# Token numbers and router bias added on TensorE, ranks moved between z's halves, b2 added in one operation

## The reference

```python
h = layernorm(x) * (1 + ca) + sa
xi = silu(h @ Win + bin)                  # 256 channels; then a scan with decay 0.9
x = x + ga * (scan(xi) @ Wout + bout)
h = layernorm(x) * (1 + cb) + sb
logits = h @ Wr + br                      # 8 experts
probs, idx = top_k(softmax(logits), 2); probs /= probs.sum()
for each row and each of its two experts e:
    t = layernorm(relu(h @ W1[e] + b1[e])) * g1[e] + be1[e]
    y = layernorm(relu(t @ W2[e] + b2[e])) * g2[e] + be2[e]
x = x + gb * (sum of probs * y)
```

## Time and profile before

| | us |
|---|---|
| three runs | 504.31, 505.99, 506.33 (median 505.99) |
| profiled execution | 503.4 |
| span of its instructions | 501.6 |
| busy in it: PE, DVE, ACT, POOL | 475.5, 452.2, 406.3, 348.3 |

### The profile page before, as it was taken

One profiled execution on the slowest core, in us unless ns is written; L12 is line 12 of the kernel. 1 busy time (PEld: TensorE's weight loads), 2 busy tenths in 40 slices (PEclk: granted clock), 3 DMA queues, 4 the chain that ended last, 5 costly groups with the idle time before them and its releaser, 6 DMA issues. The chain is left out here.

```text
span 501.6 us, 15039 instructions
## 1 busy us (share of the span) xinstructions
PE 475.5 (95%) x3083; PEld 366.6 (73%) x3083; DVE 452.2 (90%) x2245; ACT 406.3 (81%) x1118; POOL 348.3 (69%) x461
## 2 busy tenths in 40 slices
PE   7998999999999899999999999999999999999994
PEld 6454555555567688888888888888888888888851
DVE  6879999998888899899998899999999999999994
ACT  3678898988865777777887888989998889989883
POOL 1003666666767777788888878888887888888871
PEclk9999999999999999999999999999999999999998
DMA  5990511114211578988726986766667667667555
GB/s 165 313 256 18 132 50 48 43 56 106 64 43 56 136 172 163 166 246 205 192 82 160 200 221 137 204 192 185 202 183 178 186 191 207 166 181 212 189 177 167
DMA packets 80364, 78.36 MB, mean 156 GB/s; under 512 B 11433, under 2 KB 73052, under 8 KB 80276
## 3 DMA queue, kind: packets, MB, share of 16 engines
q1 hardware_dynamic: 71860, 60.48, 48.9%
q0 software_dynamic: 8416, 16.93, 9.5%
HBM read 55.20 MB, written 22.62 MB: 155 GB/s over the span
## 5 line engine op out<-in xcount | busy, mean ns | idle before, releaser
L704 POOL DMA_INDIRECT expert_rows<-rows_ring,slot x128 | 123.4, 964 | 93.2 <-issue 74.7
L732 POOL DMA_INDIRECT expert_results<-y,target x119 | 120.4, 1012 | 32.7 <-issue 28.1
L1686 PE MATMUL bank<-W,h2T 128*128 x720 | 96.4, 277 | 1.8 <-DVE wmod L1455 0.9
L1686 PEld LDWEIGHTS bank<-W,h2T 128*128 128x128 f32 x720 | 87.5, 191 | 12.5 <-issue 5.6
L1668 PE MATMUL bank<-W1hi,h3hi 128*128 x135 | 65.5, 485 | 1.3 <-DVE h3lo L1221 1.3
L949 ACT ACTIVATE v<-wmod 128x128 f32<-128x128 f32 x135 | 41.8, 310 | 29.3 <-DVE vg L1466 25.5
L1226 DVE BATCH_NORM_STATS2 stf<-h1T 128x6 f32<-128x512 f32 x90 | 59.2, 658 | 0.0
L814 ACT ACTIVATE n<-X,nm,rs 128x128 f32<-128x128 f32 x128 | 52.7, 488 | 7.1 <-DVE nm L1395 7.1
L961 ACT ACTIVATE sde<-mve,eps 128x2 f32<-128x2 f32 (+1 forms) x138 | 40.6, 295 | 17.9 <-DVE mve L1479 15.6
L1676 PE MATMUL bank<-ident_wr,h1T 128*128 128x128 f32 x360 | 54.4, 274 | 0.2 <-ACT third_rT L829 0.2
L829 ACT ACTIVATE h2T<-bank 128x512 f32<-128x512 f32 x90 | 52.7, 586 | 1.0 <-PE bank L1676 0.9
(11 more groups left out here) (253 smaller groups left out, 1172.0 us busy)
## 6 DMA issues: line engine op xcount, KB each, us to landing
shifts<-expert_shifts SPq DMA_DIRECT2D x119, 192.0 KB
hrow<-expert_rows SPq DMA_DIRECT2D x135, 65.0 KB
xi<-expert_results SPq DMA_DIRECT2D x12, 512.0 KB, 6.0
out_x<-X SPq DMA_DIRECT2D x15, 256.0 KB, 3.9
X<-in_L_attn_x SPq DMA_DIRECT2D x7, 512.0 KB, 7.4
b_ring<-b_two_parts SPq DMA_DIRECT2D x135, 4.0 KB
W1lo<-in_L_ffn_W SPq DMA_DIRECT2D x4, 512.0 KB, 5.9
expert_rows<-rows_ring,slot POOLq DMA_INDIRECT x128
```

Of the source, the lines that this page charges most:

```text
L704: nc.gpsimd.indirect_dma_start(out=rows_d, out_offset=bass.IndirectOffsetOnAxis(ap=slot[q][:, n // TOPK, n % TOPK:n % TOPK + 1], axis=0), ...
L732: nc.gpsimd.indirect_dma_start(out=results_d, out_offset=bass.IndirectOffsetOnAxis(ap=target[i % TARGETS][:], axis=0), in_=y[k], in_offset ...
L1686: ins = mm(acc, rT[i % DEPTH][:, ch * P:(ch + 1) * P], W2[:, bass.ds(e * CF + ch, 1), :], start=(ch == 0), stop=(ch == CF - 1))
```

## The change

The row in `rows` now has h first, then token number and expert, then the logits. `ident_wr` gets two zero columns between identity and `wr` (138 columns). A new table `tags` holds per row the token number, a zero and br. Two matmuls with the identity as weights add it to the product of L1768 in the banks, so that ScalarE's two copies bring token numbers and finished logits; VectorE's addition of br and its copy of the token numbers go. `max` and `max_index` read `rows` and wait for `rows_ready`; the pieces of `scale_w2` and the table that stood between logits and `max` now stand ahead of that wait. GpSimd's wait for `logit_ready` becomes one for `best_ready`. The ranks become a function; in steps 3 to 15 it is called between the halves of z, from step 16 on where they stood. `copy_sums` is one addition over 98 partitions and stands after the experts' numbers are written; two matmuls with `padding` in step 0 fill bank 4 for it. VectorE makes `tags` with a copy and two memsets in the setup and a copy of br in step 1.

```diff
+        tags = sb("tags", [P, NT, TAGS + E])
@@ ScalarE
-                    nc.scalar.activation(rows[k2][:, 0:J - 1, TAGS:], back, ACT.Copy)
-                    nc.scalar.activation(rows[k2][:, J - 1:J, TAGS:], back_last, ACT.Copy).then_inc(rows_ready, 1)
+                    nc.scalar.activation(rows[k2][:, 0:J - 1, :], back, ACT.Copy)
+                    nc.scalar.activation(rows[k2][:, J - 1:J, :], back_last, ACT.Copy).then_inc(rows_ready, 1)
@@ GpSimd
-                pool.wait_ge(logit_ready, b + 2)
+                pool.wait_ge(best_ready, b + 2)
@@ VectorE, setup
-            vec.tensor_copy(token[:], token_i[:])
+            vec.tensor_copy(tags[:, :, 0], token_i[:])
+            vec.memset(tags[:, :, 1], 0.0)
+            vec.memset(ident_wr[:, P:P + TAGS], 0.0)
@@ gains_setup
+                dve.wait_ge(gains_loaded, 80)
+                vec.tensor_copy(tags[:, :, TAGS:], br[:].rearrange("p (o e) -> p o e", o=1).broadcast_to([P, NT, E]))
@@ copy_sums
-                for rows_k in side_rows:
-                    ins = vec.tensor_tensor(w2_sums[rows_k, n, :], bank[4][rows_k, n * D:(n + 1) * D], b2_rows[rows_k, n, :], ALU.add)
+                ins = vec.tensor_tensor(w2_sums[0:side_rows[-1].stop, n, :], bank[4][0:side_rows[-1].stop, n * D:(n + 1) * D],
+                                        b2_rows[0:side_rows[-1].stop, n, :], ALU.add)
@@ VectorE, mixer_step
-                if on(s - SUMS_FROM - 1, ROUNDS):
-                    copy_sums(s - SUMS_FROM - 1)
-                if on(c, B):
-                    dve.wait_ge(rows_ready, c + 1)
-                    vec.tensor_tensor(logit[p][:], rows[k3][:, :, LOGITS],
-                                      br[:].rearrange("p (o e) -> p o e", o=1).broadcast_to([P, J, E]),
-                                      ALU.add).then_inc(logit_ready, 1)
...
-                    dve.wait_ge(logit_ready, c + 1)
+                    dve.wait_ge(rows_ready, c + 1)
...
-                    vec.tensor_copy(rows[k3][:, :, 0], token[:, tiles(c)])
...
-                    vec.tensor_copy(rows[k3][:, :, 1], besti[p][:, :, 0]).then_inc(ids_ready, 1)
+                    vec.tensor_copy(rows[k3][:, :, D + 1], besti[p][:, :, 0]).then_inc(ids_ready, 1)
+                if on(s - SUMS_FROM - 1, ROUNDS):
+                    copy_sums(s - SUMS_FROM - 1)
@@ TensorE, gains (step 0)
+                for n in range(ROUNDS):
+                    mm(bank[4][:, n * D:(n + 1) * D], ident[:], padding[:, H], start=True, stop=True)
@@ TensorE, mixer_step
-                if on(s - 3, B):
-                    acc = ...          # the ranks, here in every step
+                if on(s - 3, B) and s >= B:
+                    ranks(s, p)
...
                     mm(bank[3][:, 1:L], wv[:, 0, :], xi[q][:, 0, 0:L - 1], start=False, stop=False)
+                    if on(s - 3, B):
+                        ranks(s, p)
...
+                    if s == 2:
+                        pe.wait_ge(dve_setup, SETUP_SUMS)
                     for j in range(J):
-                        ins = mm(back[:, j, :] if j < J - 1 else back_last[:, 0, :], h2T[q][:, j * P:(j + 1) * P], ident_wr[:],
-                                 start=True, stop=True)
-                    ins.then_inc(back_done, 1)
+                        mm(back[:, j, :] if j < J - 1 else back_last[:, 0, :], h2T[q][:, j * P:(j + 1) * P], ident_wr[:],
+                           start=(j in (0, J - 1)), stop=False)
+                    first = (s - 2) * J
+                    mm(back[:, :, P:WIDE], ident[:], tags[:, first:first + J - 1, :], start=False, stop=True)
+                    mm(back_last[:, :, P:WIDE], ident[:], tags[:, first + J - 1:first + J, :], start=False, stop=True).then_inc(back_done, 1)
```

More of the change, by code:

```diff
@@ L47, in adaln_ssm_moe_kernel @@
     ROW = TAGS + D
-    TOKEN, EXPERT, H = slice(0, 1), slice(1, 2), slice(TAGS, TAGS + D)
+    H, TOKEN, EXPERT = slice(0, D), slice(D, D + 1), slice(D + 1, D + 2)
     LOGITS = slice(TAGS + D, TAGS + D + E)
@@ L128, in adaln_ssm_moe_kernel @@
         onesf = sb("onesf", [P, P])
-        WIDE = P + E
+        WIDE = P + TAGS + E
         ident_wr = sb("ident_wr", [P, WIDE])
-        ident, wr = ident_wr[:, 0:P], ident_wr[:, P:WIDE]
+        ident, wr = ident_wr[:, 0:P], ident_wr[:, P + TAGS:WIDE]
         before = sb("before", [P, P], BF16)
@@ L140, in adaln_ssm_moe_kernel @@
         token_i = sb("token_i", [P, NT], I32)
-        token = sb("token", [P, NT])
         padding = sb("padding", [P, ROW])
@@ L166, in adaln_ssm_moe_kernel @@
         RING = 6
-        rows_ring = sb("rows_ring", [P, RING, J, TAGS + WIDE])
+        rows_ring = sb("rows_ring", [P, RING, J, WIDE])
         rows = [rows_ring[:, k, :, :] for k in range(RING)]
@@ L172, in adaln_ssm_moe_kernel @@
         offs = rows_ring[:, RING - 2, 0, 0:P].bitcast(I32)
-        logit = [sb(f"logit_{q}", [P, J, E]) for q in range(2)]
         best = sb("best", [P, NT, 8])
@@ L363, in adaln_ssm_moe_kernel @@
              "scan_ready", "mix_ready", "mix_done")]
-        (x1_ready, n2_ready, t2_done, h2T_ready, back_done, rows_ready, logit_ready, best_ready,
+        (x1_ready, n2_ready, t2_done, h2T_ready, back_done, rows_ready, best_ready,
          besti_ready, hot_ready, hots_ready, carry_ready, rank_done, placed_ready, slot_ready,
          ids_ready) = [sem(n) for n in (
-             "x1_ready", "n2_ready", "t2_done", "h2T_ready", "back_done", "rows_ready", "logit_ready",
+             "x1_ready", "n2_ready", "t2_done", "h2T_ready", "back_done", "rows_ready",
              "best_ready", "besti_ready", "hot_ready", "hots_ready", "carry_ready", "rank_done",
@@ L1261, in mixer_step @@
                 if on(c, B):
-                    dve.wait_ge(logit_ready, c + 1)
+                    dve.wait_ge(rows_ready, c + 1)
                     dve.nop(nofuse=True)
                     for j in range(J):
-                        ins = vec.max(best[:, c * J + j, :], logit[p][:, j, :])
+                        ins = vec.max(best[:, c * J + j, :], rows[k3][:, j, LOGITS])
                     ins.then_inc(best_ready, 1)
@@ L1277, in mixer_step @@
                     for j in range(J):
-                        ins = vec.max_index(besti[p][:, j, :], best[:, c * J + j, :], logit[p][:, j, :])
+                        ins = vec.max_index(besti[p][:, j, :], best[:, c * J + j, :], rows[k3][:, j, LOGITS])
                     ins.then_inc(besti_ready, 1)
@@ L1688, in values, with ranks @@
                 ins.then_inc(y_done, 1)
+            def ranks(s, p):
+                acc = bank[7][:, ACC].rearrange("p (j e) -> p j e", j=J)
+                pe.wait_ge(hots_ready, s - 2)
+                if isinstance(s, int) and s - 3 in GROUP_ENDS[:-1]:
+                    pe.wait_ge(carry_ready, s - 3)
+                    mm(bank[7][:, COUNTS], ones[:], hots[p][:, J, :], start=True, stop=True)
+                if isinstance(s, int) and s - 3 == TABLE1_WRITTEN:
+                    pe.wait_ge(spread_ready, 1)
+                    mm(bank[7][:, TABLE:TABLE + 2 * P], onesf[:], spread[:].rearrange("p t i -> p (t i)"), start=True, stop=True).then_inc(spread_done, 1)
+                mm(acc, before[:], hots[p][:, 0:J, :], start=True, stop=False)
+                mm(acc, ones[:], region[:].rearrange("p (o e) -> p o e", o=1).broadcast_to([P, J, E]), start=False, stop=False)
+                for j in range(J - 1):
+                    mm(acc[:, j + 1:J, :], ones[:], hots[p][:, j:j + 1, :].broadcast_to([P, J - 1 - j, E]),
+                       start=False, stop=False)
+                if on(s - 4, B):
+                    pe.wait_ge(carry_ready, s - 3)
+                mm(acc, ones[:], hots[p][:, J:J + 1, :].broadcast_to([P, J, E]),
+                   start=False, stop=True).then_inc(rank_done, 1)
             def turn_normalised(s, q):
```

## The result

The changed kernel takes 499.98 us (median of four runs, 499.2 to 501.55) where the kernel before takes 505.21 beside it (504.31 to 506.33). The ratio is 0.9911 with an interval of 0.9884 to 0.9939: faster by 5.2 us or 0.9%, clear of the noise, where 4.5 were forecast. Now and then an execution of either kernel is slower by more than the usual scatter of the others, and medians and ratios leave such slow ones out.

What follows compares the result with a forecast made beforehand. The prediction took a circle of waits between PE and VectorE, through ACT's copies, to set the 8.43 us mixer step. Terms: 9.7 - 6.2 + 2.3 - 0.8 - 0.15 - 0.3 = 4.5 us gained, giving 501.5 us, range 498.0 to 505.4.

Steps and rivals of the forecast that it cites:

- case A: Whole kernel: the sum of the terms holds, 501.5 us, its own range 499.8 to 503.2 us; chance 0.56.
- The ranks between the halves of z: Mixer steps 3 to 15: ranks behind z's first half remove all PE waits for hots, gaining 9.7 us.
- VectorE late next: Plain mixer steps: VectorE would need 8.2 us without the lightening and be late next; with it 7.7 to 7.9.
- The pair of tags: PE, steps 2 to 15: four float32 instructions at 0.11 us each, 0.44 us a step, cost 6.2 us.
- What comes back: Passages from L1768 to L1706, steps 4 to 15: tags cover h1T wait and weight load, 0.21 us each, 2.3 us.
- case C: Gain goes elsewhere: L1706's load stays exposed (2.3 us), tags cost 0.19 each, or POOL holds; 503.5 to 506.2 us, chance 0.27.
- The wait for xi: z's first half, ten steps: ACT's copies start later, so z waits about 0.08 us a step, 0.8 us lost.
- b2 and the ends: b2 in one addition gains nothing further; tag table's memsets lose 0.15 us at the start, steps 16 and 17 0.3 us.
- GpSimd's pace: POOL: six stores from 147.60 to 155.57 take 7.97 us at its own pace, just under the new 8.1 us step.
- Rival B: PE: narrow tag matmuls cost 0.10 us a pair, then POOL's 7.97 us takes over; 498.2 us, chance 0.11.
- The expert tiles: From 166.2 us to 480 us: the stretch keeps its 313.8 us and only starts earlier; profiled execution 498.9 us.

## Why the prediction was right, and where its size was off

The side, the mechanism and case A (499.8 to 503.2 us) held. The gain was 5.2 us instead of 4.5. That 499.98 us lies near the low end of case A and 1.5 us under the 501.5 is half due to the kernel before, which took 505.21 us beside it and not 505.99.

**The ranks between the halves of z: right.** All thirteen waits are gone. The full size of a wait, idle time and 0.17 us, is seen in step 9: 1.20 us between turns and z became 0.44. The move alone gives 6.9 us at the mixer's end, and 8.1 and 8.5 with b2 in one addition, of the 9.7 on the list. The rest is VectorE being late.

**VectorE late next: right in kind, too high in size.** I gave VectorE 8.2 us a step without the lightening. Its own pace is 7.94 us, as the scans of the kernel without tags show, against 7.79 of PE. The 8.11 us with the ranks alone hold the four additions of b2 as well, and without those the mean is 7.99. So VectorE's lateness costs 7.99 - 7.79 = 0.20 us a step, where I had some 0.4, and the lightening was worth less than its role in my argument. Measured at the mixer's end, tags and lightening together lose 3.3 us.

**The pair of tags: 0.44 us forecast, 0.36 measured.** 0.11 us per instruction is right, and a second pair costs 0.45. But the first load hides behind the last stream of turning back, so the first pair costs 85.30 - 84.93 = 0.37 us, and 0.35 net in step 2. Over 14 steps that is some 1.1 us less than the 6.2.

**What comes back: 0.21 us forecast, 0.12 measured.** The wait for h1T is gone (0.10 us): h1T is ready at 84.97 and wanted at 85.30. The exposed load of the first projection is not: it takes 1.10 us beside the 1.13 of before, 1.12 without tags and 1.10 behind bf16 tags, so no kernel here covers it. The rows of PEld above show how: the loads of the tags follow each other without a gap, and the load of L1724 starts only 0.03 us before its matmul (85.27 and 85.30). A covered load starts 0.11 us before it (62.03 and 62.14 in the rows below). That is what case C had in its first half, and it took 0.09 of the 0.21 us. 11 times 0.09 is 1.0 us less than the 2.3.

**The wait for xi: 0.8 us forecast and there, but as much comes back beside it.** Rows of ACT, PEld and PE around z, first of the changed kernel, then of the kernel without tags, where xi is ready early:

```profile
86.76 0.69 ACT L849 ACTIVATE xi<-bank,bcol 128x512 f32<-128x512 f32 x1
87.50 0.30 PEld L1755 LDWEIGHTS bank<-xi,wz 128*128 128x128 f32 x2
```

```profile
61.25 0.69 ACT L850 ACTIVATE xi<-bank,bcol 128x512 f32<-128x512 f32 x1
62.03 0.30 PEld L1758 LDWEIGHTS bank<-xi,wz 128*128 128x128 f32 x2
62.14 1.02 PE L1758 MATMUL bank<-xi,wz 128*128 128x512 f32 x2
```

In the changed kernel xi is ready at 86.76 + 0.69 = 87.45, the load starts at 87.50 and the matmul at 87.53, and z's first projection takes 0.94 us to its second. In the other the load starts 0.11 us before the matmul, and the projection takes 0.86 us. So xi costs the 0.08 us a step that I gave it, though the table of waits doesn't list it. But z took 91.97 - 91.02 = 0.95 us before as well, there behind the bf16 ranks, and moving the ranks gives that back. I compared with a clean z and not with the z of the trace. What the moved ranks do cost is 0.04 us in the turns behind them, which I had not listed: 13 x 0.04 = 0.5 us.

**b2 and the ends.** b2 at nothing was right for this kernel. The tables put the start 0.10 us back (0.15 forecast). From the start of step 15 to the count matmul 0.22 us were lost. The forecast for this stretch was a gain of 0.2 (a wait of 0.48 + 0.17 less one pair) less the drain's 0.3, so the drain cost about 0.4.

Put together: 9.7 - 5.0 + 1.3 - 0.5 - 0.1 - 0.4 = 5.0 us, beside 5.10 at the mixer's end. Three errors of up to 1 us went partly against each other (+1.1 for the pair, -1.0 for what comes back, +0.8 - 0.5 around z), so it is luck that the sum was better than its terms.

**GpSimd's pace: not 7.97 us.** Rival B held its gain back by it. But one of the six stores had waited 0.69 us for VectorE, as this row of before shows, and the kernels without tags and with bf16 tags run steps of 7.79 and 7.90 us:

```profile
149.24 0.96 POOL L704 DMA_INDIRECT expert_rows<-rows_ring,slot  x1 [0.69 <-DVE logit L1255]
```

**The expert tiles** keep their time only as a mean. The predicted 498.9 us for the profiled execution missed (501.55), by the scatter of that stretch.

## What to carry to other kernels

When two engines wait for each other in a circle, move the small consumer behind independent work that is longer than the wait. Then ask for each further edit which engine it loads and which is late by then: here the tags load the engine that has just become the bound, by 0.36 us a step, to spare one whose lateness costs 0.20. The cost of a small float32 matmul followed its weight load here, not its columns, so one with 10 columns (0.22 us) costs a quarter of one with 512 (0.86 us). And compare each piece with the piece as it stands in the trace, not with its clean form.

## What the hardware showed beyond that

A 10-column float32 matmul costs 0.22 us in a row of its kind and a bf16 one 0.027 us, eight times less, so three bf16 parts are cheaper than one float32. Behind a run of bf16 matmuls the first float32 matmul comes late by 0.04 us (turns) to 0.09 us (z). A strided bf16 copy of 192 elements was 0.97 us long on VectorE and 1.04 us on ScalarE; one of 1536 was 1.17 and 1.77 us long. The same program's DMA-fed stretch of 336 us varied by 2.7 us between three executions of the changed kernel and by 5.5 us between two of the kernel before, as much as the whole gain.
